# First attention of a four-layer network: softmax denominators by token, outputs by head, and side work placed after every second block of keys

## What is computed

```
x = x + attention0(layernorm(x), ctx)      # 16 heads of 64, context of 1024 tokens
q = x_normed @ Wq, k = rope(ctx_normed @ Wk), v = ctx_normed @ Wv
w = clip(exp(q k^T / 8), e^-11, e^11)      # no row maximum is taken in this layer
out = (w v) / sum_k(w)   per head;   x += out @ Wo (+ bias, added earlier)
```

## Time and profile before

| what | value |
|---|---|
| median of 3 runs | 2766.04 us (2760.65 to 2767.31) |
| profiled execution, its time / span in the profile | 2766.01 us / 2764.3 us |
| layer 0's 16 steps, first scores to last `weigh` | 89.8 to 534.7 us |
| granted TensorE clock, mean of the run | 0.876 |

### The profile page before, as it was taken

The page is one execution under the profiler, slowest core; times in us unless marked ns, Lnnn a source line. Parts: engine busy times, 40 slices in busy tenths (PEclk is TensorE's granted clock), DMA queues, the critical chain, the costliest instruction groups (busy, mean ns, idle before and its releaser), DMA issues.

```text
span 2764.3 us, 34540 instructions
## 1 busy us (share of the span) xinstructions
PE 2154.2 (78%) x13832; PEld 1500.8 (54%) x13832; DVE 1379.5 (50%) x2156; ACT 757.4 (27%) x1164; POOL 700.7 (25%) x757
## 2 busy tenths in 40 slices
PE   2789898659958888885985787399678888469994
PEld 2445444248944444443883554299534544368883
DVE  4688888733136667675314543222465564412123
ACT  2444444212122333331112322000124445211111
POOL 3212121033320010001223221355411010154443
PEclk8899999869978999997996777599879999689997
DMA  4011000048920000001571000389300000078883
GB/s 142 16 30 32 23 26 18 8 158 284 316 98 8 11 15 10 8 8 41 182 254 37 16 12 5 118 311 328 131 12 18 10 11 3 22 267 294 294 293 103
DMA packets 96559, 274.66 MB, mean 99 GB/s; under 512 B 14128, under 2 KB 44592, under 8 KB 96016
## 3 DMA queue, kind: packets, MB, share of 16 engines
q0 software_dynamic: 45168, 206.99, 21.6%
q1 hardware_dynamic: 51232, 65.46, 7.6%
HBM read 239.50 MB, written 20.32 MB: 94 GB/s over the span
## 4 chain that ended last, share of the span: by engine, by line
PE 54%; DVE 20%; issue 10%; DMA 6%; ACT 5%; POOL 4%; another core or an unknown queue 0%; SPq 0%; DVEq 0%; POOLq 0%; ACTq 0%
PE psum L1976 11%; PE psum L277 9%; PE psum L1999 7%; PE psum L742 5%; PE psum L722 5%; DVE plain L888 5%; DVE plain L1513 3%; PE psum L1343 3%; PE psum L1316 2%; DMA plain<-sorted_x 2%; DMA plain<-in_l_en,plain 2%; PE psum L1360 2%; ACT plain L1028 2%; DVE plain L861 2%; PE psum L315 1%
## 5 line engine op out<-in xcount | busy, mean ns | idle before, releaser
L1976 PE MATMUL psum<-plain 128*128 128x128 f32 x3904 | 492.4, 279 | 10.4 <-DMA plain<-in_l_shared 8.6
L1976 PEld LDWEIGHTS psum<-plain 128*128 128x128 f32 x3904 | 484.8, 195 | 22.5 <-issue 9.7
L277 PE MATMUL psum<-split 128*128 128x256 f32 (+1 forms) x1728 | 379.9, 373 | 71.1 <-DVE split L350 9.8
L277 PEld LDWEIGHTS psum<-split 128*128 128x128 f32 x1728 | 286.8, 210 | 202.0 <-issue 115.9
L2100 POOL DMA_INDIRECT plain<-in_l_ffn,plain x274 | 259.9, 949 | 401.6 <-PE psum L1999 379.4
L1999 PE MATMUL psum<-plain 128*128 128x256 f32 x1160 | 303.8, 385 | 33.2 <-DVE plain L2065 30.6
L1028 ACT ACTIVATE plain<-psum 128x1024 f32<-128x1024 f32 x224 | 227.4, 1023 | 359.7 <-PE psum L742 246.1
L888 DVE TENSOR_TENSOR plain<-plain 128x1024 f32<-128x1024 f32 x200 | 265.6, 1328 | 12.4 <-ACT plain L1028 9.4
L722 PE MATMUL psum<-plain 128*64 128x512 f32 x896 | 241.8, 640 | 32.3 <-DVE plain L895 27.4
L742 PE MATMUL psum<-split 64*128 64x512 f32 x1536 | 237.0, 432 | 37.0 <-DVE plain L861 30.0
L1056 POOL TENSOR_TENSOR plain<-plain 128x512 f32<-128x512 f32 x48 | 67.7, 1410 | 673.1 <-DMA plain<-plain 669.9
(11 more groups left out here) (176 smaller groups left out, 2278.9 us busy)
## 6 DMA issues: line engine op xcount, KB each, us to landing
plain<-plain SPq DMA_DIRECT2D x192, 64.0 KB
plain<-sorted_x SPq DMA_DIRECT2D x76, 128.0 KB
sorted_y<-plain SPq DMA_DIRECT2D x76, 128.0 KB
plain<-in_l_w SPq DMA_DIRECT2D x20, 256.0 KB
plain<-in_l_ffn,plain POOLq DMA_INDIRECT x274
plain<-in_ctx SPq DMA_DIRECT2D x8, 512.0 KB, 5.9
plain<-in_l_wo SPq DMA_DIRECT2D x28, 128.0 KB, 2.0
plain<-in_l_tab SPq DMA_DIRECT2D x3, 1024.0 KB
```

Of the source, the lines that this page charges most:

```text
L277: m = t.e.matmul(out, lhs[x], rhs[y], start=(first and n == 0), stop=(last and n == 2), skip_group_check=skip)
L1976: m = t.e.matmul(K.bank(b)[:, 256 * z + P * f:256 * z + P * f + P], ws[:, f, c0:c0 + 128], xt[:, k, :], start=(f == 0 and k == 0 and z == ...
```

## The change

It touches layer 0's attention. Denominators come out by token: 8 matmuls with 128x128 pieces of the running sum as weights and one column of ones, then one reciprocal of 128x8. Bank 4 is copied to `OT` undivided by ACT, at the start of the next step. The output is made per head, in two halves: 8 matmuls of 64 rows into two banks per half; DVE multiplies each with its head's reciprocal and adds it to x in one instruction, 8 of 128x256 per step in place of 4 additions. The order of pieces becomes

and all engines take them after odd blocks: with the new weights 2, 2, 3 and 4 pieces after blocks 1, 3, 5 and 7. The diff, cut to its core (plain forwarding of arguments left out):

```diff
             weights = [0.5] * (n > 0) + prep[:2] + [1.8] * (n > 0) + prep[2:]
+            if n and not own:
+                v = 1.5 if n + 1 < self.n and self.values(n + 1)[0] else 0.0
+                p = 1.5 if n + 1 < self.n else 0.0
+                weights = [p, p, p, v, 2.0, 0.9, 0.2, v, 0.2, 0.9, 0.2]
+            elif not own:
+                v = 1.5 if self.values(1)[0] else 0.0
+                weights = [1.5, 1.5, 1.5, v, 0.2, v, 0.2, 0.2]
...
+                two = paced(weights, total, [(kt + 2) / nk for kt in range(0, nk, 2)])
+                self.pace.append([x for n in two for x in (0, n)])
...
+    elif n:
+        copied(n - 1)
+        for _ in range(4):
+            next(g, None)
+            yield
         divide(n - 1)
         yield
+        output(n - 1, 0)
         yield
+        for _ in range(3):
+            next(g, None)
+            yield
+        output(n - 1, 1)
         yield
     yield from g
...
     before, last = A.values(n)
+    if n and not A.own:
+        query(n)
+        yield
+        for i in range(2):
+            if before:
+                values(*before[i])
+            yield
+            split(n, i)
+            yield
+        if A.steps[n][1] == 1:
+            resplit(A.steps[n][0])
+        yield
+        return
...
@@ tensor_attention64, divide @@
+        if not own:
+            for i in range(4):
+                for h in range(2):
+                    m = t.e.matmul(K.bank(b)[:, 2 * i + h:2 * i + h + 1], A.SA[n % 2][:, h, 128 * i:128 * i + 128],
+                                   K.ONES[:, 0:1], start=True, stop=True)
...
+    def output_heads(n, half):
+        p = A.steps[n][0]
+        t.wait_ge("av_copied", (L, n))
+        t.wait_ge(f"wo{p % 2}", (L, p))
+        bs = [RB.get(), RB.get()]
+        t.bank(*bs)
+        for i in range(2):
+            q0 = 128 * (2 * half + i)
+            for h in range(2):
+                r = slice(64 * h, 64 * h + 64)
+                m = t.e.matmul(K.bank(bs[h])[:, 256 * i:256 * i + 256], A.OT[r, q0:q0 + 128], K.WO64[p % 2][r, :],
+                               start=True, stop=True)
+        m.then_inc(*t.up("out", L, n, half))
...
@@ vector_attention64, divide @@
+        if not own:
+            if n:
+                v.wait_ge("x_added", v.made["x_added"])
+            v.wait_ge("sums", (L, n))
+            v.e.reciprocal(K.RCP[:, 0:8], K.bank(K.at.get(("sums", L, n), 0))[:, 0:8]).then_inc(*v.up("recip", L, n))
+            return
...
+    def output_heads(n, half):
...
+        for h in range(2):
+            if h or half == 0:
+                v.wait_ge("x_added", v.made["x_added"])
+            for i in range(2):
+                q = 2 * half + i
+                x = K.X[:, 4 * b + q, :]
+                m = v.e.scalar_tensor_tensor(out=x, in0=K.bank(banks[h])[:, 256 * i:256 * i + 256],
+                                             scalar=K.RCP[:, 2 * q + h:2 * q + h + 1], in1=x, op0=ALU.mult, op1=ALU.add)
...
@@ scalar_attention64 @@
+    def copied(n):
+        if n:
+            s.wait_ge("out", (L, n - 1, 1))
+        s.wait_ge("weighed", (L, n, nk - 1))
+        s.e.activation(A.OT, K.bank(4), ACT.Copy).then_inc(*s.up("av_copied", L, n))
...
@@ sync_attention64, load of the next Wo @@
-                y.wait_ge("out", (L, n - 2, 3))
+                y.wait_ge("out", (L, n - 2, 3 if A.own else 1))
```

More of the change, by code:

```diff
@@ L582, in side64, with prepare64 @@
         tail()
-def prepare64(n, A, keys, values, split, late, query, own, rowmax, shift):
+def prepare64(n, A, keys, values, split, late, query, own, rowmax, shift, resplit):
     if n >= A.n:
@@ L711, in prepare @@
     def prepare(n):
-        return prepare64(n, A, keys, values, nothing, late, query, own_keys, rowmax, shift)
+        return prepare64(n, A, keys, values, nothing, late, query, own_keys, rowmax, shift, nothing)
     def weigh(n, kt):
@@ L791, in tensor_attention64 @@
     for n in range(A.n):
-        side = side64(n, A, divide, prepare, output, tail)
+        side = side64(n, A, nothing, divide, prepare, output if own else output_heads, tail)
         attend(n, side)
@@ L795, in tensor_attention64 @@
     divide(n)
-    output(n)
+    if own:
+        output(n)
+    else:
+        output_heads(n, 0)
+        output_heads(n, 1)
 def vector_attention64(v, K, A):
@@ L876, in prepare @@
     def prepare(n):
-        return prepare64(n, A, keys, nothing, split, late, query, own_keys, rowmax, shift)
+        return prepare64(n, A, keys, nothing, split, late, query, own_keys, rowmax, shift, resplit)
     def add(n, kt):
@@ L909, in divide @@
         v.e.tensor_tensor(A.OT, K.bank(4), A.OT, ALU.mult).then_inc(*v.up("divided", L, n))
+    def output_heads(n, half):
+        b = A.steps[n][1]
+        v.wait_ge("biased", v.seen["biased"])
+        v.wait_ge("recip", (L, n))
+        v.wait_ge("out", (L, n, half))
+        banks = K.at.get(("out64", L, n, half), (0, 0))
+        for h in range(2):
+            if h or half == 0:
[5 more added lines that the diff above has]
+                                             scalar=K.RCP[:, 2 * q + h:2 * q + h + 1], in1=x, op0=ALU.mult, op1=ALU.add)
+                m.then_inc(*(v.up("x_added", L, n, half, h) if i else v.up("x_added")))
     def output(n):
@@ L1041, in scalar_attention64 @@
     for n in range(A.n):
-        side = side64(n, A, nothing, prepare, nothing, tail)
+        side = side64(n, A, copied, nothing, prepare, nothing, tail)
         attend(n, side)
         run(side, 1000)
+    if not own:
+        copied(n)
 def gpsimd_attention64(g, K, A):
@@ L1074, in prepare @@
     def prepare(n):
-        return prepare64(n, A, keys, nothing, split, late, nothing, nothing, nothing, nothing)
+        return prepare64(n, A, keys, nothing, split, late, nothing, nothing, nothing, nothing, nothing)
     def add(n, kt):
@@ L1147, in sync_attention64 @@
     sync_load_out64(y, K, L, 1)
-    run(prepare64(0, A, keys, *[nothing] * 7), 1000)
+    run(prepare64(0, A, keys, *[nothing] * 8), 1000)
     if L == 0:
@@ L1151, in sync_attention64 @@
     for n in range(1, A.n):
-        run(prepare64(n, A, keys, *[nothing] * 7), 1000)
+        run(prepare64(n, A, keys, *[nothing] * 8), 1000)
 def nothing(*_):
```

42 lines of the change are left out of this document (25 added, 17 removed).

## The result

The changed kernel takes 2753.76 us (median of 15 runs, 2739.89 to 2762.74), the kernel before, run beside it, 2766.24 (15 runs, 2752.97 to 2776.17). The ratio is 0.9948, interval 0.9931 to 0.9964: 10 to 19 us faster, 14 in the middle. A second set of the same comparison gave 2749.39 against 2763.67, ratio 0.9946 (0.9923 to 0.9969). The direction and the range held; 26.5 us were forecast.

A forecast was written before the change was run, and what follows sets the result against it. With PE (89%) and DVE (82%) near full, gains come from their mutual waits or work taken off both. Savings of 21.1 (13 steps), 4.3 (step 14) and 1.1 (layer end), 26.5 off 2766.01, give 2740 us; range 2733 to 2758.

The forecast's parts named there:

- 13 middle steps: Layer 0's steps 1 to 14, by projection starts: from 28.12 to 26.5 us each, 21.1 us saved.
- step 14: Layer 0's step without values to project: from 29.8 to 25.5 us, 4.3 us saved.
- step 15 to the transposes: Layer 0's last step: keeps its loop of 2.97 us per block, four additions become four fused ones, 0 saved.
- from there to the last addition: End of layer 0, from the transposes to the last addition: 12.3 us to 11.2, 1.1 us saved.
- PE's terms: PE's work per step: denominators 2.05 us, outputs 2.0, with scores, weights times values and projections 25.7 in all.
- rival A: PE's half outputs do not pair and take 1.9 us each, making PE the bound at 27.5 per step: 2756 us; chance 0.12.
- DVE's terms: DVE per step: 5.70 us removed (reciprocal, multiplication, four additions), 4.12 added (small reciprocal, eight fused instructions), gaining 1.6.
- the new wait of 0.7: PE waits some 0.7 us per step at the next first scores, for the low part of the keys' second half.
- the second is touched at its start. I add 0.1: DVE's second running sum beside GpSimd's two tensor_tensors: touched only at its start, 0.1 us added, giving 26.5 per step.
- The walk: One layer 0 step followed from its first scores across engines: next first scores at 26.4 us, PE needing 25.7.
- Rival B: DVE's loop is longer, through paired waits of fused instructions or a slowed running sum (up to 1.1): 27.1 per step, 2748 us; chance 0.17.
- Rival C: TensorE's clock falls at the denominators each step, PE needing 29.6 us: slower, 2782 us; chance 0.05.

The follow-up runs named there:

- the version with the early half output: Changed kernel with denominators, reciprocal and first half output after block 3 instead of block 5: 2737.38 us, 0.9894 against the kernel before.
- the kernel with the old spread: Changed kernel's arithmetic with pieces in the order and pace of the kernel before: 2817.5 us, 1.0167; with denominators two projections later: 2765.18 us, 1.0005.

## Why the prediction was half right

The forecast had 26.5 us off. In the profiled pair the first layer gave 16.7 (all times in us):

| part | forecast | measured | from |
|---|---|---|---|
| up to step 1 | 0 | 0.5 | 118.81, 118.27 |
| 13 middle steps | 21.1 | 13.7 | 365.5, 351.83 |
| step 14 | 4.3 | -0.2 | 29.78, 29.96 |
| step 15 to the transposes | 0 | 4.2 | 29.60, 25.35 |
| from there to the last addition | 1.1 | -1.6 | 12.3, 13.9 |

**PE's terms held.** Denominators 1.95 of 2.05; half outputs 8 records in 1.13, of which the next group overlaps part (1.0 forecast), so float32 matmuls of 64 rows pair and rival A is out; PE busy 25.5 against 25.7. The rows of a related form, corrected for the overlap of groups, gave PE's step within 0.2.

**DVE's terms held.** Reciprocal 0.20, four fused instructions in 1.79 (4 x 0.484 forecast), the copy on ACT hidden, the wait of 1.07 gone, the new wait of 0.7 at the first scores where it was expected.

**The step that failed** is "the second is touched at its start. I add 0.1": the term for GpSimd in the loop. The walk had GpSimd finished 14 us into the step. But VectorE holds GpSimd up too. GpSimd's four operations take 1.38, 1.62, 2.06 and 1.73 (1.28 undisturbed), and end 15.1 us into the step (267.60 less 252.47), so the second running sum (266.39, 2.29) starts while the last of them runs, and within the loop: 1.07 more between two exponentials. The walk's later points follow, each late: exponential 5 at 16.3 (268.77 less 252.47) for 15.1, exponential 7 at 23.5 for 22.75, the next first scores at 27.1 for 26.4. Rival B had this mechanism, its row of 1.1 and its 27.1 per step, and its sign came (PE waits 1.6 us per step, over 1.2); its other half, fused instructions that wait for each other, did not. It was given 0.17 and ought to have been the forecast, since the position of those operations could have been walked like everything else. The check of the walk against the old step does not speak for the 0.1, since there the slowed sum was counted in full. The kernel with GpSimd's part made small shows the term alone: 25.88 in the mean (116.32 to 452.81), so it costs 1.2 per step. The walk without it gives 26.4, 0.5 too much: 0.4 of this lies in DVE's pieces, which from the sum's end at 271.65 to the clip at 274.11 take 2.5 us for 2.87. That the step missed by 0.6 and not by 1.1 is luck, since the two errors partly cancel.

The Trainium skill's page "SBUF — State Buffer", section "🎯 Summary: rules for kernel authors", says of DVE with two SBUF inputs beside a GpSimd operation that reads SBUF that "the second one to issue **fully blocks** until the first finishes", and advises to schedule whichever is off the critical path. The trace agrees, instruction by instruction. In the change's 13 steps 22 running sums start while a GpSimd instruction runs, and each ends 1.07 to 1.09 us after that instruction's end, while undisturbed they take 1.22. Above, GpSimd's last instruction ends at 267.60 and the sum of 266.39 at 268.68. The other way round, 37 GpSimd instructions start during a clip or a running sum, and 36 of them end 1.12 to 1.15 after it. In all 22 cases GpSimd's instruction had started during the clip just ahead of the sum: it runs behind the clip, and the sum stands still for 1.2 us. So the price to forecast with is 1.1 us for each sum met in this way, and not 0.1 for a touch at the start. The advice fits the version with the early half output: the fused instructions, which read PSUM, kept 0.47 to 0.49 in all 49 cases in which they started beside GpSimd.

**Step 14** has no values to project, and I let it save their time. But its end was held by DVE: both low parts (1.29) fell behind block 7 with four fused instructions, the wait before the last weights was 1.8, at the first scores 1.3 and at the next denominators 1.25, and the scores behind took 2.62, in part at half clock, for 1.66. **Step 15** was put at nothing, wrongly: the reciprocal of 3.36 stood at its head too, and PE waited 2.58 behind it. Without it the last clip comes 16.9 us after the first scores instead of 18.8, and two running sums of three (3.74) no longer stand ahead of the layer norm. They come back behind it (528.65, 2.48), together with the last eight weights times values at half clock (3.68 for 1.94): that is the loss of 1.6 at **the end of the layer**, where 1.1 were to be won. The three last terms add to 2.4 where 5.4 were forecast.

The drift behind layer 0 is not the change's, as far as the repeated profiles tell, and layer 0's 14.2 to 16.7 us over the four pairs of profiles lie within the ratio's 10 to 19. Rival C did not come in the change (granted clock 1.00 in the plain steps), but the kernel with the old spread shows that the clock can fall in this stage.

**What carries.** The arithmetic alone gained nothing (28.8 per step, or 32.1 with the denominators in a bad place), the order alone lost 80 us, both together gained 14, and a further move of the same pieces 15 more: in this stage, with two engines over 80% busy, where a piece stands decided more than what it costs. So walk one step on every engine, GpSimd too, and put down the slowed duration on both sides, for GpSimd as for VectorE.

## To carry to other kernels

When a loop over exponentials, clips and sums is held by VectorE, find what GpSimd does during it, and put VectorE's work that reads PSUM there rather than clips and sums over SBUF operands. Look at the last steps of a list by themselves: pieces that fall out there leave others together, and what is moved behind a layer's end is paid there. Where a term is 0.1 or 1.1 by the position of one instruction, work that position out on every engine before choosing.

## What the hardware did that was not expected

- GpSimd and VectorE shut each other out rather than share: a running sum of 128x1024 that starts beside a GpSimd instruction ends 1.07 to 1.09 us after it (22 of 22 in the change, 13 of 13 before), so 2.3 for 1.22; GpSimd's 128x512 takes up to 2.25 for 1.28. Fused instructions that read one operand from PSUM kept 0.47 to 0.49 in the same place (49 of 49).
- TensorE's clock fell behind short waits in some steps and not in others. In the kernel with the old spread, with waits of 1.7 to 2.9 us at the clip and, in most steps, of 1.07 at the one-column matmuls, nine of thirteen projections behind them ran partly at half clock (mean granted clock 0.91); with the second wait gone, three of fourteen did (0.96). Behind a wait of 7.68 us the clock was at half.
- Two executions of one kernel part by 6 us, and two of the changed kernel by 10, in layers that the change does not touch.
